# A decoder layer's steady step reordered: expert-gate logits taken from the cross-attention products, the key and value product moved to slot 4

## The reference, cut to what matters

```python
x = layernorm(x + self_attention(x))           # 16 query heads of 16, one shared key and value head
x = layernorm(x + cross_attention(x, context)) # 120 context rows, one head, with a mask
logits = x @ Wg.T                              # 8 experts
comb = two largest of softmax(logits), divided by their sum + 1e-9
x = layernorm(x + sum over experts e of comb[e] * (a * sigmoid(b) @ Wo.T + bo))   # (a, b) = x @ W1[e].T + b1[e]
```

## Time and profile before

| what | us |
|---|---|
| median of 3 runs | 1400.23 (1399.9 to 1410.04) |
| the profiled execution, its own time | 1407.59 |
| its span, first to last instruction | 1405.2 |
| attention's steady steps, blocks 7 to 31 | about 163 to 713 |
| draining and tables | about 732 to 838 |
| expert tiles, then combining | about 839 to 1264, then to 1405 |

### The profile page before, as it was taken

How to read it: one execution, slowest core, us unless ns; L and a number is a source line. 1 busy time by engine, 2 the same in 40 slices (tenths; PEclk the granted TensorE clock), 3 DMA queues, 4 the chain that set the end, 5 groups by cost and what they waited for, 6 DMA issues and landing times.

```text
span 1405.2 us, 30425 instructions
## 1 busy us (share of the span) xinstructions
PE 1272.8 (91%) x7734; PEld 901.7 (64%) x7735; DVE 1105.5 (79%) x3115; ACT 746.3 (53%) x1740; POOL 637.3 (45%) x917
## 2 busy tenths in 40 slices
PE   6988999999989999999998759899999999997997
PEld 4443555556555555555554447688888888877997
DVE  1566798888988889898897656678888888876997
ACT  1235677787777877777776412233222322323555
POOL 3011245554555545455454523665465565551333
PEclk7998999999999999999999759999999999998999
DMA  6647497897987879777574784888788788877885
GB/s 187 174 94 142 100 213 177 219 213 201 219 178 195 183 205 213 167 175 162 136 145 174 259 297 83 129 135 131 123 138 136 122 137 135 131 107 240 281 274 179
DMA packets 194871, 242.73 MB, mean 173 GB/s; under 512 B 21712, under 2 KB 144592, under 8 KB 190544
## 3 DMA queue, kind: packets, MB, share of 16 engines
q1 hardware_dynamic: 159392, 153.70, 45.8%
q0 software_dynamic: 26128, 54.94, 22.8%
q10 hardware_dynamic: 9248, 32.86, 7.1%
HBM read 142.46 MB, written 120.24 MB: 187 GB/s over the span
## 4 chain that ended last, share of the span: by engine, by line
PE 68%; DVE 9%; issue 7%; DMA 7%; ACT 4%; POOL 3%; SPq 2%; DVEq 0%; ACTq 0%; POOLq 0%
PE psHb L1445 7%; PE psHb L1441 6%; PE psHb L1442 6%; PE psO L644 6%; PE psS L751 5%; PE psB L673 4%; PE psHa L1441 4%; PE psHa L1442 4%; PE psHa L1445 4%; PE psT L761 4%; DVE negmax L1065 3%; DMA qstack<-q_parts 2%; PE psHa L1498 2%; PE psX L1465 2%; PE psA L633 2%
## 5 line engine op out<-in xcount | busy, mean ns | idle before, releaser
L1065 DVE TENSOR_REDUCE negmax<-psS 128x2 f32<-128x512 f32 x512 | 350.5, 687 | 101.2 <-PE psS L751 83.4
L904 ACT ACTIVATE probs<-psT 128x512 f32<-128x512 f32 x512 | 303.2, 598 | 164.3 <-PE psT L761 149.1
L1523 ACT ACTIVATE sig<-hb 128x512 f32<-128x512 f32 x135 | 85.4, 633 | 297.1 <-DVE hb L1598 243.7
L1406 POOL DMA_INDIRECT g_rows<-g,slot x135 | 211.9, 1569 | 37.3 <-issue 34.8
L751 PE MATMUL psS<-kstack,qstack 96*128 96x256 bf16 x1024 | 195.9, 274 | 30.9 <-DVE kstack L1163 12.0
L761 PE MATMUL psT<-qstack,kstack 99*128 99x512 bf16 x512 | 194.9, 383 | 4.5 <-ACT probs L904 4.5
L751 PEld LDWEIGHTS psS<-kstack,qstack 96*128 96x128 bf16 x1024 | 93.6, 104 | 90.3 <-DVE negmax L1065 24.9
L503 POOL DMA_INDIRECT lists<-x,slots x128 | 128.6, 1005 | 33.9 <-issue 30.1
L644 PE MATMUL psO<-probs,vaug 128*32 128x512 f32 x1024 | 139.0, 615 | 0.4 <-ACT probs L904 0.4
L1607 DVE SCALAR_TENSOR_TENSOR g<-g,xe,sig 128x512 f32<-128x512 f32 x135 | 101.6, 752 | 26.1 <-ACT sig L1523 11.7
L1441 PE MATMUL psHb<-w_hi,xet_hi 128*128 x270 | 118.6, 439 | 0.0
(11 more groups left out here) (210 smaller groups left out, 2799.4 us busy)
## 6 DMA issues: line engine op xcount, KB each, us to landing
qstack<-q_parts SPq DMA_DIRECT2D x192, 128.0 KB
g_rows<-zero_rows ACTq DMA_DIRECT2D x20, 1024.0 KB, 6.8
xe<-lists SPq DMA_DIRECT2D x135, 132.5 KB
rows<-g_rows SPq DMA_DIRECT2D x32, 512.0 KB, 5.0
q_parts<-qpart SPq DMA_DIRECT2D x32, 384.0 KB
sums<-x SPq DMA_DIRECT2D x32, 264.0 KB
x2in<-sums SPq DMA_DIRECT2D x32, 264.0 KB, 3.4
xt<-in_x_t SPq DMA_DIRECT2D x32, 256.0 KB
```

The source lines that it names most:

```text
L904: nc.scalar.activation(probs[:, u % PT, :], psT[:, u % 2, :], ACT.Exp, scale=SELF_SCALE).then_inc(sm["exp_done"], 1)
L1065: v.tensor_reduce(negmax[:, b1.s2, 2 * hp:2 * hp + 2, c], psS[:, u % 2, :].rearrange("p (h k) -> p h k", h=2), AX.X, ALU.max, negate=True) ...
L1406: pool.indirect_dma_start(out=dram["g_rows"], out_offset=bass.IndirectOffsetOnAxis(ap=slot[:, o.s4:o.s4 + 1], axis=0), in_=g[:, o.s4], in_ ...
```

## The change

The gate's columns (wg less each expert's mean) are appended to the cross products: `keymap` grows from 120 to 128 columns per block, so the cross scores yield x1's part of the logits; the context's part is a new product of transposed context rows (`ctxt`, a new load of 120 KB per block) with `wgc`, made beside the weights' transposes in slot 9, copied by ACT into eight extra columns of `ctxv`, so that the cross output yields its part. y2 then carries 256 + 8 columns, the last eight being the logits before scaling. The transposes of x2, its copy, the gate product and the logits' copy go. POOL multiplies the negative maximum by the second norm's scale (`scale_max`), ACT's gate exponentials take the scale as an operand.

Because the cross output now needs 264 columns a half, it takes both banks in slot 14. Bank B's round becomes: query projection (2), keys' and values' product (4, after the slot's pair), transposed maxima (7, after the pair), weights' transposes (9), cross output (14). The keys' copies move to slot 6 on ACT and DVE, their split to ACT's slot 7 and DVE's slot 8. ACT's gate exponentials move to slots 8 and 9, one half each, the second norm to slots 10 and 11, one half each. The second norm's statistics are spread over slots 0 and 1, its moments move to slot 2. The counts use `psO`. In draining steps the gating runs in slots 1 to 15 and rows are sent at the end of the same step, so the pipeline has 38 steps.

```diff
-        for n in range(B + 7):
+        for n in range(B + 6):
...
+            if active(b6) and draining(t):
+                dispatch(b6, 0)
+                dispatch(b6, 1)
...
-        bank_b = {"q_projected": ("q_rest", 0, 1, 1), "x2_transposed": ("x2t_copied", 6, 1, 1),
-                  "gate_scored": ("gate_link", 6, 7, 1), "cprob_transposed": ("cprobt_copied", 5, 1, 1),
-                  "kv_projected": ("k_rest", 0, 1, 1), "counted": ("slot_link", 6, 3, 1)}
+        bank_b = {"q_projected": ("q_rest", 0, 1, 1), "kv_projected": ("k_rest", 0, 1, 1),
+                  "m_transposed": ("m_copied", 2, 1, 1), "cprob_transposed": ("cprobt_copied", 5, 1, 1),
+                  "cross_out": ("y2_ready", 5, 1, 1)}
...
+                    wait(pe, f"ctxt_loaded{b5.s2}", 16 * b5.half + 16)
+                    for k in range(DC):
+                        last = mm(psB[0:SC, S:S + E], ctxt[:, b5.s2, k, :], wgc[:, k, :],
+                                  start=k == 0, stop=k == DC - 1)
...
+                if u == 4 and active(t):
+                    bank_read(bank_b, t, "kv_projected")
...
+                if u == 7 and active(b2):
+                    wait(pe, "m_split", done(b2))
+                    bank_read(bank_b, t, "m_transposed")
...
-                if u == 4 and active(b6) and not draining(t):
+                if u in (10, 11) and active(b6) and not draining(t):
...
+                if u in ((6,) if draining(t) else (8, 9)) and active(b6):
...
-                if u == 12 and active(t):
+                if u == 6 and active(t):
                     wait(act, "kv_projected", done(t))
...
-                if u == 13 and active(t):
+                if u == 7 and active(t):
 
                     wait(act, "k_rest", done(t))
...
+                    v.tensor_copy(x1[:, b5.s2, :, D:D + E], both[:, :, SC:SC + E]).then_inc(sm["raw_copied"], 1)
```

More of the change, by code:

```diff
@@ L392, in step @@
                              ).then_inc(dram["zeros_stored"], 16)
[L393 to L398, removed]
+            if active(t.back(7)) and t.n <= B + 1:
+                store_x2(t.back(7))
             b = t.back(3)
@@ L428, in step @@
                 load_experts(t)
+            if active(t.back(6)) and draining(t):
+                store_x2(t.back(6))
         pipeline(sp, step)
@@ L482, in expert_constants, with scale_max, rstd @@
                            pad[:, E:, :]).then_inc(dram["pads_stored"], 16)
-        def rstd(b, var, mv, vare, nmean, out, shift, ready, more=None):
+        def scale_max(b):
+            wait(pool, "rstd2_ready", 4 * b.n + 2)
+            pool.tensor_tensor(gneg[:, b.s2], uneg[:, b.s2], rstd2[:, b.s2], ALU.mult).then_inc(sm["rstd2_ready"], 1)
+        def rstd(b, var, mv, vare, nmean, out, shift, ready, more=None, per=3):
             wait(pool, var, done(b))
@@ L526, in step @@
                 expert_constants()
-            if active(b7):
-                if not active(t):
-                    wait(pool, "slots_ready", done(b7))
+            late = active(b7) and t.n <= B + 1
+            if late:
                 dispatch(b7, 0)
@@ L680, in step @@
                         for k in range(DC):
-                            last = mm(psA[:, c * SC:(c + 1) * SC], x1t[:, b5.s2, k, c * P:(c + 1) * P],
-                                      keymap[:, k, bass.ds(b5.n * SC, SC)], start=k == 0, stop=k == DC - 1)
+                            last = mm(psA[:, c * (SC + E):(c + 1) * (SC + E)], x1t[:, b5.s2, k, c * P:(c + 1) * P],
+                                      keymap[:, k, b5.n, :], start=k == 0, stop=k == DC - 1)
                     last.then_inc(sm["cross_scored"], 1)
[L684 to L705, removed]
                 if u == (0 if draining(t) else 8) and active(b4):
@@ L818, in clear_rows, with norm @@
                               ).then_inc(dram["rows_cleared"], 16)
-        def norm(x, rs, shift, y, b, ready, name):
-            wait(act, ready, done(b, 3))
-            for c in range(QC):
-                last = nc.scalar.activation(x[:, b.s2, c, 0:D], y[:, b.s2, c, :], ACT.Identity,
+        def norm(x, rs, shift, y, b, ready, name, per=3, half=None):
+            wait(act, ready, per * b.n + 3)
+            for c in range(QC) if half is None else (half,):
+                last = nc.scalar.activation(x[:, b.s2, c, 0:D], y[:, b.s2, c, 0:D], ACT.Identity,
                                             scale=rs[:, b.s2, c:c + 1], bias=shift[:, b.s2, c:c + 1])
-            last.then_inc(sm[name], 1)
+            if half != 0:
+                last.then_inc(sm[name], 1)
         def copy_att(b, g):
@@ L987, in split_max, with own_rstd @@
                 v.tensor_tensor(part[:, 2], r, part[:, 1], ALU.subtract).then_inc(sm["m_split"], 1)
-        def own_rstd(b, mv, vare, out, shift, var, ready, k):
+        def own_rstd(b, mv, vare, out, shift, var, ready, k, per=3):
             if k == 0:
```

339 lines of the change are left out of this document (195 added, 144 removed).

## The result

The changed kernel takes **1561.1 us** (median of 4 runs, 1553.41 to 1564.98) against 1400.43 for the kernel before beside it: a ratio of **1.1118**, 95% interval 1.1073 to 1.1162, slower by 11%. I had forecast 1454 and a range up to 1470. The profiled execution took 1564.98, span 1562.8.

The account below looks back on a forecast made before the run. PE and DVE, both nearly full and tied slot by slot, bound the 21.8 us step; 2.0 - 0.8 + 0.8 makes 23.8. Sum 52 + 1.5 - 1.5 + 1.8 = +54 on 1400.23: 1454 us, range 1384 to 1470.

Parts of the forecast that it names:

- the three waits: PE waits from bank B's new round: 0.36 at slot 4, 0.8 at slot 7, 1.4 at slot 9.
- the walk: Tracing one steady step instruction by instruction from the query projection's start Q: 23.8 us instead of 21.8.
- my 54: Forecast total change in us: 52 + 1.5 for steps, -1.5 for load waits, +1.8 at the start, draining 0.
- Slot 10, 2.0 later: Slot 10's score product starts at Q + 13.95 against 11.93, held by ACT's copy of the transposed maxima.
- 0.8 won back: Slot 10 to next slot 0: DVE loses the keys' rest and split, so 6.63 us against 7.44.
- 0.8 lost: Slot 0 to x1's transposes: POOL's addition chain allows them at 8.96 after slot 10; PE arrives at 8.15.
- long possible: Claim that products of slots 10 and 11 could start early, DVE's maxima, 2.11 apart, pacing the step there.
- I leave the clock alone: Granted clock assumed unchanged, no cost: PE was busy 14.12 of 18.00 us with short waits at 1.00.
- Rival 3: The clock falls as well: a tenth of PE's step at 1.2 GHz, 2.0 more a step, 1508 us; chance 0.04.
- Draining, taken as 0: Last block's savings against POOL's transfers ahead of the next step's scale: bounds -6 to +9, taken as 0.
- no waits for the loads: Steps that had waited longer for loads into qstack lose that wait under the longer step: about -1.5.
- my 1.8: Start: two small PE products and three DVE operations on the weight-folding chain, between 0.5 and 2.8, taken as 1.8.

Follow-up runs that it names:

- run with filled waits: The changed kernel with 24 matmuls that compute nothing ahead of slot 9's transposes and 18 ahead of slot 13's scores: 1503.58 us.

## Why the prediction was wrong

The direction was right, and so were the three waits. What failed, largest first: the clock, which I left alone (58 us); slot 10, put 2.0 later in a step, which came 3.0 later; and draining with what follows the last projection, put at 2 (the last of the 26 steps, and nothing for draining), which cost 16. From block 5's projection to block 31's I had 50 (1.5, 25 steps of 2.0, less 1.5 for loads); the trace has 137.3, of which the clock is 58 and the walk at full clock 79 (649.3 against 570.1). With the start's 2.4 more this closes: 58 + 29 + 14 + 2.4 = 103 of the 103.6 by which the profiled execution's difference of 157.6 passed my 54.

The run with filled waits shows the walk at full clock (its Q at 598.40), beside the numbers that I gave:

| step of the prediction | given | measured |
|---|---|---|
| wait of the keys' product, slot 4 | 0.36 | 0.45 |
| wait of the maxima's transpose, slot 7 | 0.8 | 0.68 |
| wait at slot 9, in the changed kernel | 1.4 | 1.61 |
| slot 9's transposes | Q + 11.44 | Q + 12.37 |
| slot 10 | Q + 13.95 | Q + 14.97 |
| slot 10 to the next slot 0 (7.44 before) | 6.63 | 7.30 |
| x1's transposes, wait for POOL's chain | 0.8 | 0.0 |
| step at full clock | 23.8 | 24.7 |
| clock | nothing | 2.2 a step |
| draining | 0 (-6 to 9) | 14 (16.0 from the last projection on, less the last step's 2.0) |

*Slot 10, 2.0 later: 3.0, the term of the walk that I sized wrong.* The chain through ACT was the right one; 0.9 of the missing 1.0 are there by slot 9. ACT's list had no gap, as I said, but its first item began 0.42 later, since PE came to slot 6 that much later, and most items were longer, 0.5 in all. In the step at 607.89, which answers to the earlier trace rows:

```profile
616.36 0.60 ACT L927 ACTIVATE probs<-psT 128x512 f32<-128x512 f32 x1 [0.60 <-PE psT L766]
...
619.19 0.39 ACT L887 ACTIVATE gexp<-y,gneg,rstd 128x8 f32<-128x8 f32 x1
...
619.86 0.24 ACT L897 COPY mrows<-psB 96x128 bf16<-96x128 bf16 x1
```

Half the gate exponentials, with the scale as an operand, take 0.67 (619.19 to 619.86) and not 0.47; the cross exponentials 0.88 (616.85 to 617.73) and not 0.77.

*"0.8 won back" and "0.8 lost" behind slot 10: wrong in mechanism, without weight in the sum.* From slot 10's product to x1's transposes it was 8.96 before, I forecast 8.96, and the run with filled waits has 8.84 (7.30 + 1.54). But I took the 0.8 off a stretch that DVE paces only as far as slot 13. In the kernel before slot 10 starts at 306.75 and the next slot 0 at 314.19; between them stand the keys' product, slot 11 and slot 13:

```profile
307.19 1.03 PE L719 MATMUL psB<-xt,wk 128*96 128x256 f32 x4
...
308.87 0.38 PE L751 MATMUL psS<-kstack,qstack 96*128 96x256 bf16 x2
...
310.03 0.39 PE L751 MATMUL psS<-kstack,qstack 96*128 96x256 bf16 x2
```

In the run with filled waits slots 10, 13 and the next 0 start so:

```profile
613.37 0.38 PE L764 MATMUL psS<-kstack,qstack 96*128 96x256 bf16 x2
...
616.53 0.39 PE L764 MATMUL psS<-kstack,qstack 96*128 96x256 bf16 x2
...
620.67 0.39 PE L764 MATMUL psS<-kstack,qstack 96*128 96x256 bf16 x2 [0.44 <-DMA qstack<-q_parts]
```

Slot 10 to slot 13 takes 3.28 and 3.16, slot 13 to the next slot 0 takes 4.16 and 4.14. Behind slot 13 PE goes through its own products without a bracketed wait until slot 0, so DVE's two pieces were not in the way; there the 0.49 for the keys gave way to 0.44 for the loads, which I had ruled out. I had also read the earlier trace rows wrongly: slot 11's product was not "long possible", it started at 308.87, behind the keys' and values' product and 0.41 ahead of its maximum. PE's product and DVE's stretch were equally long. Without the product PE reaches slot 13 early and waits 1.39: idle time, and no time won. (In the run with filled waits part of the added matmuls stands in that wait.) The chain for x1, which I charged with 0.8, is as long as in the earlier trace rows, but PE came later than I thought:

```profile
626.42 1.64 POOL L554 TENSOR_TENSOR y<-att,xres 128x512 f32<-128x512 f32 x1 [9.06 <-DVE att L998]
...
631.80 0.19 POOL L513 TENSOR_TENSOR shift<-nmean,rstd 128x2 f32<-128x2 f32 x1
```

From 626.42 to the shift's end 5.6 pass, 5.8 in the kernel before.

*"I leave the clock alone": the step that cost most.* Rival 3 had the mechanism and a price of 2.0 a step, for a tenth of PE's time at 1.2 GHz, at a chance of 0.04. In the step shown two pieces, 6.8 of 27.6 us, ran there; at some 1.3 to 1.4 each this makes 27.4 of 24.7. Over the 26 steps the clock is 58 us (2.2 a step) and the walk 79 (3.0, from a mean of 21.9), together the 137 that the steps have grown by. I took one row as leave to drop it: 14.12 of 18.00 us busy at a clock of 1.00. The changed kernel has the same share, 10.35 of 13.10, in the stretch ahead of a fall, so that row could not rule a fall out. The Trainium skill (TensorE: Matmul & The Clock Gate, "A second HAM failure mode: psum-queue depth-cycling") tells of short idles between groups of matmuls that send the clock to and fro; the trace agrees, with the pieces at 0.51 and 0.50 shown above.

*Draining, taken as 0: 14.* I priced POOL's transfers, which are what they were the earlier trace rows:

```profile
L523 POOL DMA_INDIRECT lists<-x,slots x128 | 128.3, 1002 | 64.1 <-DVE slots L1086 34.2
```

I left out that the counts, moved from slot 15 to slot 7, stand on PE ahead of everything else of the step while DVE still makes the hot rows: 21.1 us of waits in five steps. From the last score product to the first expert product it is 98.7 against 89.0; the other 6 come ahead of that product, in the last steps, which still run as the steady ones do. The run with the counts moved back won 6.1. What part of the 9.7 is those waits is not shown: the granted clock over that stretch was lower as well, 0.70 against 0.78.

*Loads and start.* I expected no waits for the loads. The changed kernel has one of 0.5 from 280 to 850; in the run with filled waits, whose steps are shorter, slot 0 waits for them 16 times from 280 to 820, 9.5 us in all. The start cost 4.2 by block 5 against my 1.8.

What stays open is which pattern of idle makes the clock fall. Filling the waits raises it, and so does work in slot 11; waits added to the kernel before leave it. Neither the sum of the waits nor PE's busy share over a stretch, as read here, separates the two.

## What to carry to other kernels

Before moving a product to an emptier slot, ask what it covers where it stands: on an engine that goes in order, work is also the time that another engine is given. Two waits that cost little apart can be dear together, when they lie in one stretch and the clock falls behind it; price a clock fall from the trace (here 1.3 to 1.4 us for each piece of 3.4) and give it a real chance as soon as a change adds idle time to an engine that now runs without a break. A wait moved early in a step holds up everything queued behind it, so in a pipeline's tail only the last step should go early.

## What was unexpected of the hardware

The granted clock fell to 1.2 GHz although PE's longest single idle in the step was 1.61 us; with the rows back in bank A it fell in a step whose longest was 0.86, with 2.4 us of waits in all. It held at 1.00 in the kernel before with waits added, with 3.5 us of waits in a step and one of 1.17. Matmuls that compute nothing, 42 of them in a step, made the kernel 58 us faster.
